# A recommendation tower on one core: ScalarE's order in the table look-ups, one queue for all tables, and the zero products around the last product

## The reference, cut to what matters

```
e = stack([tbl_f[ids[:, f]] for f in range(26)], axis=1)        # 512 x 26 x 128
combined = concatenate([e, x[:, None, :]], axis=1)              # 512 x 27 x 128
interact = einsum('bfd,bgd->bfg', combined, combined)
z = interact[:, i < j]                                          # 351 pairs a row
h = maximum(concatenate([z, x], axis=1) @ W_top1 + b_top1, 0)   # 479 -> 512
h = maximum(h @ W_top2 + b_top2, 0)                             # 512 -> 256
y = h @ W_top3                                                  # 256 -> 1
```

## Time and profile before

| | us |
|---|---|
| median of 3 runs | 114.54 (114.31 to 116.4) |
| the profiled execution | 115.43 |
| its span, first to last instruction | 113.6 |
| TensorE busy in the span | 100.8 |
| ScalarE, VectorE, GpSimd busy | 49.1, 53.2, 68.6 |

### The profile page before, as it was taken

How to read it: one execution, slowest core, us unless ns; L and a number is a source line. 1 busy time by engine, 2 the same in 40 slices (tenths; PEclk the granted TensorE clock), 3 DMA queues, 4 the chain that set the end, 5 groups by cost and what they waited for, 6 DMA issues and landing times.

```text
span 113.6 us, 3435 instructions
## 1 busy us (share of the span) xinstructions
PE 100.8 (89%) x1538; PEld 84.9 (75%) x1538; DVE 53.2 (47%) x108; ACT 49.1 (43%) x73; POOL 68.6 (60%) x72
## 2 busy tenths in 40 slices
PE   6957999999975999999998969999999989883992
PEld 6943788888854788688778759887989789682890
DVE  1019989999949685980010083116220443007130
ACT  4422553994374759529942151015331313500122
POOL 3277777777778777877777777777677730000000
PEclk9999589999997699999999999999999999999999
DMA  2999955947962899411211221221222210000000
GB/s 77 349 358 398 369 192 163 265 141 239 319 239 48 244 389 344 135 46 46 72 49 52 59 68 46 52 72 49 52 46 74 53 46 0 6 6 0 6 0 1
DMA packets 6001, 14.68 MB, mean 129 GB/s; under 512 B 1889, under 2 KB 2913, under 8 KB 5858
## 3 DMA queue, kind: packets, MB, share of 16 engines
q1 hardware_dynamic: 3650, 9.22, 22.4%
q0 software_dynamic: 2048, 4.20, 14.4%
q10 hardware_dynamic: 288, 1.05, 2.6%
HBM read 14.45 MB, written 0.00 MB: 127 GB/s over the span
## 4 chain that ended last, share of the span: by engine, by line
PE 68%; DMA 10%; ACT 8%; issue 6%; DVE 5%; SPq 0%; DVEq 0%
PE look_ps L286 27%; PE gram_ps L321 12%; PE look_ps L352 10%; PE look_ps L362 7%; DMA ids_wide<-ids_look_dram 6%; PE turn_ps L307 5%; DMA table<-tbl_dram 4%; PE look_ps L332 3%; ACT apart L573 3%; ACT onehot L576 3%; DVE onehot L481 2%; DVE dots L489 2%; PE look_ps L344 1%; PE look_ps L371 1%; PE look_ps L377 1%
## 5 line engine op out<-in xcount | busy, mean ns | idle before, releaser
L262 POOL DMA_INDIRECT rows<-tbl_dram,ids_rows x64 | 67.7, 1058 | 22.6 <-issue 19.2
L286 PE MATMUL look_ps<-onehot,high 128*128 128x512 f32 x88 | 35.6, 421 | 4.4 <-ACT onehot L576 2.4
L286 PE MATMUL look_ps<-onehot,low 128*128 128x512 f32 x88 | 34.5, 415 | 0.0
L481 DVE TENSOR_SCALAR onehot<-ids_wide,row_ids 128x1024 fp32r<-128x1024 int32 x37 | 25.8, 748 | 9.0 <-DMA ids_wide<-ids_look_dram 6.7
L286 PEld LDWEIGHTS look_ps<-onehot,high 128*128 128x128 f32 x88 | 17.1, 197 | 9.7 <-ACT onehot L576 3.2
L286 PEld LDWEIGHTS look_ps<-onehot,low 128*128 128x128 f32 x88 | 18.1, 205 | 3.9
L559 ACT CAST high<-table 128x1024 fp32r<-128x1024 f32 (+1 forms) x10 | 11.2, 1136 | 8.8 <-DMA table<-tbl_dram 8.8
L489 DVE STREAM_TRANSPOSE dots<-gram_ps 128x352 f32<-128x352 f32 (+2 forms) x12 | 5.6, 465 | 19.7 <-PE gram_ps L321 19.7
L471 DVE TENSOR_TENSOR low<-table,high 128x1024 fp32r<-128x1024 f32 (+1 forms) x10 | 13.1, 1319 | 2.5 <-ACT high L559 2.5
L321 PE MATMUL gram_ps<-vecs 128*27 128x27 f32 x1024 | 12.8, 195 | 1.6 <-ACT vecs L597 0.7
L321 PEld LDWEIGHTS gram_ps<-vecs 128*27 128x27 f32 x1024 | 10.9, 108 | 3.8 <-issue 1.1
(11 more groups left out here) (37 smaller groups left out, 53.5 us busy)
## 6 DMA issues: line engine op xcount, KB each, us to landing
ids_wide<-ids_look_dram SPq DMA_DIRECT2D x5, 512.0 KB, 4.0
table<-tbl_dram SPq DMA_DIRECT2D x4, 640.0 KB, 5.5
table<-tbl_dram SPq DMA_DIRECT2D x4, 512.0 KB, 10.4
table<-tbl_dram ACTq DMA_DIRECT2D x2, 512.0 KB, 5.3
rows<-tbl_dram,ids_rows POOLq DMA_INDIRECT x64, 3.5
w_sb<-w_dram SPq DMA_DIRECT2D x1, 1024.0 KB, 8.5
w_sb<-w_dram SPq DMA_DIRECT2D x1, 512.0 KB, 7.6
x_rows<-x_dram SPq DMA_DIRECT2D x1, 256.0 KB, 10.0
```

The source lines that it names most:

```text
L262: nc.gpsimd.indirect_dma_start(rows[:, t * NG + i, :], None, tables[GATHER_FIELDS[i]], bass.IndirectOffsetOnAxis(ap=ids_rows[:, t * NG + i ...
L286: mm = nc.tensor.matmul(look_ps[:, j % 2 * 2 + f, :], weights, onehot[:, (STEP0[j] + k) % RING, f * BATCH:(f + 1) * BATCH], start=(name == ...
L481: nc.vector.tensor_scalar(onehot[:, q % RING, :], ids_wide[:, j % WIDE_HELD, :], row_ids[:, kind(j), k:k + 1], None, ALU.is_equal).then_in ...
```

## The change

Three edits. First, the transfers of tables 0 and 1 leave ScalarE's queue for SyncE's, behind the wide ids of couple 0 and ahead of those of couple 1. Second, in ScalarE's list the one-hot tile of couple 2 goes ahead of the high part of table 7, and the second one of couple 3 ahead of the high part of table 9. Third, CODE_SHIFT goes from 11 to 9 and the last `keep_clock` from 4 to 3.

```diff
-CODE_SHIFT = 11
+CODE_SHIFT = 9
...
             wide_dma(0)
+            table_dma(0)
+            table_dma(1)
             wide_dma(1)
...
-            keep_clock(4)
+            keep_clock(3)
...
-            for i in range(2):
-                act.dma_start(part(table, i), looks[i].rearrange("(p k) d -> p k d", p=P)).then_inc(table_landed[i], 16)
...
             make_high(6)
+            make_hot(2, 0)
             make_high(7)
-            make_hot(2, 0)
             save_look(2)
             make_high(8)
             make_hot(3, 0)
+            make_hot(3, 1)
             make_high(9)
-            make_hot(3, 1)
```

## The result

| | before | after |
|---|---|---|
| median of the runs of one series, us | 115.47 (4 runs, 114.31 to 119.03) | 111.50 (4 runs, 110.96 to 112.05) |
| ratio after to before | | 0.971, 95% interval 0.963 to 0.979 |
| the profiled execution / its span | 115.43 / 113.6 | 111.41 / 109.6 |
| spans at a mean granted clock of 1.0 (of before: runs beside the experiments) | 111.2, 111.6, 111.8, 112.0 | 109.1, 109.7 |

The change is faster by 2.9%, where 108.9 us had been forecast: the profiled execution is 2.5 us above that. Medians here are over all runs of a series; ratios leave out the runs in which a kernel took a slower state. The clock fell twice in the profiled execution of before and once in that of after: their spans differ by 4.0 us, those at a clock of 1.0 only by 1.5 to 2.9.

What follows compares the result with a forecast made beforehand. TensorE, busy 100.8 of 113.6 us, was taken as the bound, losing time to waits and clock dips. 113.6 - 5.75 (look-ups) - 0.75 (zero products) = 107.1 of span, with 1.83 around it 108.9 us; range 107.3 to 111.5.

Steps and rivals of the forecast that it cites:

- So table 3 keeps 12.37: Start, on the one queue: table 3 lands at 12.37 as before, so couple 0's copy starts 2.55 us earlier, at 16.8.
- The wide ids: Start: couple 0's wide ids, issued at 1.21, land at 5.2 instead of 8.0, by the median transfer of 4.0 us.
- From the wide ids to table 3: SyncE's queue at the start: transfers land 1.41 us apart, from the wide ids at 5.2 to table 3 at 12.37.
- a last gather that lands in time: GpSimd: ids come in 3.5 us, so the last gather lands at 92.1, before the transposes at 92.6: no wait.
- that rival: Couple 3: table 7 comes later than 4.96 us after issue, each us costing a us; 110.9 with 2 us; chance 0.08.
- Couple 2's tile ahead of table 7's cast: ScalarE's order: TensorE no longer waits 2.12 us for couple 2's one-hot tile; the couple takes 7.29 us.
- The zero products: TensorE near the end: the code gap moves behind the third zero product, winning 0.75 us; ends 0.3 and 0.94.
- The second swap: ScalarE, couple 3's second one-hot tile ahead of table 9's cast: TensorE waits 0.2 and 0.5 us in couple 4.
- Slower: Rival: on one queue the early transfers follow each other at 4.0 us, table 3 lands at 25.2; 121.7 us, chance 0.03.
- The queue edit does nothing: Rival: couple 0's wide ids still land at 8.0, 3.25 us won at couple 2's copy; 111.4 us, chance 0.05.
- The clock: Rival: TensorE's clock falls after the new gap before step 7, costing up to 2.0 us; 110.9 us, chance 0.05.

Runs made afterwards that it cites:

- the one with the wide ids beside: Changed kernel with couple 0's wide ids on ScalarE's queue and all tables on SyncE's: 111.83 us, ratio 0.971.
- the best kernel: Changed kernel with table 7's transfer early, couple 0's one-hot tile ahead of table 3's cast, second swap undone, gathers not held: 108.34 us, ratio 0.941.

## Why the prediction was wrong

**The step that failed** is "So table 3 keeps 12.37". It came at 14.63, 2.26 us late, and couple 0's copy was 2.32 late. Along the rest of the sum this hardly changes: 2.34 at couple 1's copy, 2.3 and 2.2 at those of couples 2 and 3, 2.6 at the end of the look-ups, 2.5 at the end of the span. The failing term was the one that I had myself named as the weak one; its place in the sum was right, its size not.

It was wrong in two pieces. *The wide ids* came at 6.59 instead of 5.2, 1.39 us. I had taken the median landing of transfers that run later; in the eight profiled executions that have it and tables 0 and 1 on SyncE's queue the first one-hot tile began between 5.73 and 7.15. While it moves, the transfer engines are busy at a low rate. Here are the windows of the changed kernel, then of the kernel with the gathers held (the last columns: granted clock, share of the transfer engines, GB/s):

```profile
3.00:4.00 1.00, 1.00 (x7) 1.00 (x7) 0.00 (x0) 0.00 (x0) 0.85 (x1) 1.00 1.04 127
4.00:5.00 1.00, 1.00 (x6) 1.00 (x6) 0.00 (x0) 0.00 (x0) 0.84 (x1) 1.00 0.89 201
```

```profile
3.00:4.00 1.00, 1.00 (x7) 1.00 (x6) 0.00 (x0) 0.00 (x0) 0.00 (x0) 1.00 0.90 184
4.00:5.00 1.00, 1.00 (x6) 1.00 (x6) 0.00 (x0) 0.00 (x0) 0.00 (x0) 1.00 0.89 299
```

The same two microseconds of before moved 379 and 346 GB/s, with a table's transfer beside the wide one. The held kernels had their wide ids at 5.81, inside the others' spread, so the gathers are not shown to be what delays this piece.

*From the wide ids to table 3* it took 8.04 us, where the forecast had 7.2. This piece is the gathers': in the changed kernel and in the runs with the queue alone, with the second swap undone, with table 7 early and with two zero products fewer, it is 8.04, 7.82, 7.85, 7.57 and 7.69 (from the first one-hot tile to table 3's cast); in the two runs that hold the gathers behind the wide ids it is 6.66 both times. That is 0.9 to 1.4 us. Up to table 3's landing, the gathers' packets are 312 to 380 KB in the five and 60 and 64 KB in the two. The Trainium skill, "DMA: Bandwidth & Descriptors", section "Queues, rings and completion order", says that each transfer engine takes turns between the queues that have work for it; by that rule a gather takes time from a table though it is issued elsewhere, and these runs agree.

**What was overlooked.** The forecast took from the early ids only the benefit, a last gather that lands in time. It used a table 3 that the gathers hadn't delayed and an end that they hadn't made wait. The runs show these as alternatives: with the gathers held, the look-ups end at 53.33, as forecast, and the last transposes wait 1.42 us; with the gathers early there is no such wait, and table 3 is cast at 13.30 to 14.97 instead of 12.47. A third thing stood between: with table 7 tied to couple 1's end, the gain at the start was lost again in couple 3 (the held run and the one with the wide ids beside). I had priced that rival at a microsecond for a microsecond with a chance of 0.08; it needed 6.9 us instead of 4.96 and the clock fell on top. Nor did the forecast price the first of the two dips of the clock, which its base for couple 0's copy, 19.35, contains. Without that fall the copy came at 17.88 and 17.99 on the old queues, so that even a table 3 on time, with the copy at 16.96, is worth about 1.0 us there and not 2.55.

**What held.** Couple 2's tile ahead of table 7's cast: the wait of 2.12 is gone, 7.26 us for the couple. The zero products: from the end of the look-ups to the end of the span it takes 53.7 us after and 54.5 before, 0.8 less (forecast 0.75), and the stop ended 4.62 us after the product's start (forecast 4.6). On this the Trainium skill, "Runtime: NRT & Kernel Launch", section "Instruction fetch mechanics", has the crossing of a code block mostly hidden; the 1.86 us of before, and the 2.20 us that eight instructions fewer bring back, do not agree. That code is what is missing was an inference; the traces bear it out by place and by time. The place: in tile 0's second product 33, 29 and 25 matmuls follow the stop with CODE_SHIFT 11, 9 and 7 (the order alone, the changed kernel, two zero products fewer), and four matmuls with their weight loads are the eight instructions of two zero products. In the run with table 7 early and the gathers held, the stop inside the last product and the one behind the zero products lie 122 matmuls, as many weight loads and 12 instructions of zero products apart, 256 in all. With two zero products fewer, the one inside the last product is as far ahead of the place that was forecast: 118 matmuls, as many weight loads, 12 instructions of zero products and 8 more. The time: each page counts 12 packets on the queue for instructions, of 16 KB, and the stops of the last tile end 1.3 to 1.6 us after such a packet: it runs from 101.71 to 102.86 before (the stop ends at 104.34), from 98.40 to 99.68 in the changed kernel (101.03), from 96.74 to 97.62 with two zero products fewer (98.98). No other packet moves between 97 and 101.03 in the changed kernel. Whose list a packet carries the profile does not say.

**Smaller terms.** The second swap was priced at a loss of 0.7. With table 7 early, couples 3 and 4 take 21.35 and 21.38 us with it and 20.83 without: 0.5. In the changed kernel it came out even, since without it couple 3 waits 0.42 for a tile. **Slower** was refuted as priced: the spacing of tables 2 and 3 is 1.77 us in the changed kernel (12.86 to 14.63) and 1.33 with the gathers held (11.14 to 12.47), not 4.0. **The queue edit does nothing** was priced at 111.4 with a chance of 0.05, and the profiled execution took 111.41. Its steps come near too: 3.25 us won at couple 2's copy (measured 3.50), nothing in couples 3 and 4 together (measured 0.31 lost, 21.79 against 21.48). Its condition did not hold: the wide ids came at 6.59 and not at 8.0, and a late table 3 took back what they had won. That its number is met is in part luck. **The clock** did fall ahead of step 7 (0.5 from 9.3 to 12.8, behind a wait of 1.90), but step 7's tile would have been as late at the full clock, so by itself that did not set the copy.

**Left open:** why table 7 landed 6.9 and 7.0 us after its issue in two executions, and 3.8 to 5.6 in the eight others with that wait. The traces narrow it: the landing counts 16 increments, and in the two late ones 15 and 14 of them had come by 29.30, the last at 31.56. Without the queue edit, where the gathers were not held, 15 had come by 30.59 and the last at 32.32, so holding the gathers is not shown to be the reason. Nor is the spread of the first wide ids, 5.73 to 7.15, explained. Only one execution of each kernel has a trace. Nor was the best kernel split further: how much each of its edits gives is known only for table 7 and, by the couples, for the second swap.

## What to carry to other kernels

When a transfer is moved, list everything else that the move sets free, and price each of those both ways: the gathers that start earlier end earlier, and they also take transfer time from what the path waits for. A work item that waits for nothing late (couple 2's one-hot tile) belongs ahead of one that does; that needed no faster transfer and gained more than the queue did. But it holds only where the other's data really are late: the second swap cost 0.5 us once table 7 came early. And a gain at the start is carried to the end only if the next late transfer can be issued earlier too: look for the wait in front of its issue.

## What the runs showed of the hardware

The granted clock of TensorE fell to 0.5 of full speed near the start in some executions and not in others of nearly the same list: ahead of the first product it had idled 1.90 and 2.46 us in the two on the one queue that fell, 1.75 us or less in those that didn't; but without the queue edit it also fell behind an idle time of 0.84 followed by short ones. In the kernels with tables 0 and 1 on ScalarE's queue couple 0's copy came at 17.9 or 18.0 without the fall and at 19.0 to 19.35 with it: 1.0 to 1.5 us.

A stop that waits for nothing named shows up inside tile 0's products in ten of the thirteen profiled executions (0.61 us in the changed kernel, 1.34 with the order alone, 0.81 in the run with two zero products fewer, 0.18 in the best). It was no term of the sum, since before had none longer than 0.2 there. Its length does not go by the end of the look-ups alone: with the zero products alone it is 0.40 though they end at 59.60, and with the second swap undone, where they end at 55.09, there is none.
